# A gated delta-rule layer on one core: the score products take turns with the tile's products and transposes over three PSUM banks

## The chip, the cores and the metric

The kernel runs on one core of one Trainium2 chip. The metric is the device time of one execution in microseconds (us). The kernel before took 4402.71 us, the median of three runs (4402.53 to 4403.26).

## The reference, cut to what matters

The input is `x`, four batches of 1024 tokens with 512 features, in float32. It is normalised, `xn = layernorm(x)`, and two branches work on it:

```
g = silu(ffn(xn))                     # router, two projections, gated MLP
s = attn(xn)                          # below
out = x + s * g

qkvz = xn @ w_qkvz.T                  # 8 key heads, 16 value heads, all of width 128
q, k, v = silu(causal_conv4(q, k, v)) # four taps along the tokens
q, k = q / |q|, k / |k|
S = 0
for each token t:                     # delta rule, one 128x128 state S per value head
    S = S * exp(g_t)
    delta = (v_t - k_t S) * beta_t
    S = S + k_t (outer) delta
    o_t = (q_t * scale) S
s = rmsnorm(o * silu(z)) * norm_weight @ w_out.T
```

## The kernel before, in words

The kernel has two phases. `feed_forward` (the first 1124 us or so) computes the gate `g`, the transposed `xn` (`xt_scratch`) and the decay rates, and leaves them in DRAM. `attention`, the phase that the change touches, computes the rest.

**Tiles, chunks, units.** The heads are worked on in two groups of 4 key heads and 8 value heads. Within a group each batch is cut into tiles of 256 tokens: 32 tiles over all, which this text numbers 0 to 31. A tile has two chunks of 128 tokens, and a chunk has two units of 4 value heads (2 key heads). That is 128 units, four in each tile: units 4q to 4q+3 belong to tile q. The first two units of each batch and group are "fresh": their state is zero, and they skip the steps `recall` and `query`.

**The tile's work on TensorE.** `pe_product` (L1036) multiplies a column block of weights with the tile, in four steps over the contraction: 16 products for the key, query and value heads (L1048) and 4 for `z` (L1052). In float32 each step stands in the trace as two matmuls, so that one product is 8 of them. A product of a key, query or value head lands in a PSUM bank, and the convolution reads it from there: `act_lead` (L1071) writes the first tap, and three times `dve_conv` (L1078) adds a tap. Only then is the bank free. After the convolution and a silu come transposes: `pe_keys` (L1097), `pe_queries` (L1152), `pe_back` (L1138; the keys again, once GpSimd has scaled them at L1132) and `pe_values` (L1181). Each of these is emptied by one step of ScalarE or VectorE.

**Two banks in turn.** The list `fills` has these 30 steps of a tile in their order: 20 products and 10 transposes. Step number i goes to bank i modulo 2, and `bank_for` (L1020) makes it wait until the step two places before it has been emptied. From the first value product on, products and transposes alternate, so that in this stretch each product goes to the same bank as the product before it.

**The scores.** For each unit `pe_scores` (L1234) multiplies keys with keys and keys with queries into a bank of its own, `b_a` (bank 3): 8 matmuls in the trace, at L1244 and L1245. It waits for the keys' second transposes of its tile (`kt_sb`), for the queries' silu, and for the scores of the unit before to be emptied (`kq_sb`). `dve_scores` (L1253) empties the bank into the single buffer `kqm`. It waits for `dve_lower` (L1285) and `dve_attend` (L1292) of the unit before, since they read `kqm`; and `dve_attend` of unit n writes one of three buffers `pt`, so that it waits for `pe_answer` (L1556) of unit n-3. Between scores and lower stand the decays: a scan (L1262) and an exponential on ScalarE (L1270).

**The chains.** From the lower scores of a unit its inverse is built by doubling: GpSimd and ScalarE split the matrix in two fp16 parts (L1297, L1305, L1311), `dve_start` (L1366) starts the chain, and six rounds follow of `pe_level`, `dve_level` (L1378), `pe_merge` and `act_merge` (L1402), then `error`, `first`, `second` and `third`; `dve_third` (L1459) ends it. All their matmuls are short fp16 ones, issued by the helper `each_head` (L1345). Even and odd units have a bank and a chain each (chain 0 and chain 1), and a chain takes its units one after the other. The core of a unit follows: `recall` (L1468), `query` (L1491), `eps` (L1516), `learn` (L1530), `answer` (L1556), and at last `turn` (L1607) and, once in a chunk, `out` (L1622, 8 steps into the bank `b_o`).

**What sets the order.** Each engine's program is written out by `planned` (L813), a list scheduler. It gets lanes (lists whose order is fixed), a duration for each step and, from `after` (L1711), what each step waits for. It runs through a made-up time and lets each engine take, of the steps that are ready, the one with the longest path of steps behind it. On TensorE the lane "pe tile" holds the tiles' products and transposes, and the lane "pe build" the scores; the planner is free in how it puts the two and the chains together. On the chip each engine then runs its list strictly in this order and waits on semaphores.

Some waits tie the tiles to the units: the first tap of the query heads (`act_lead`, query head 0 of tile q) waits until the `query` step of the last unit of tile q-2 is done, since both use `qt[q % 2]`; the silu of `z` waits for the gated output of tile q-2.

Of the kernel before, what the change touches and what calls it, by code (L numbers as in the profile page):

```python
# [29 lines left out]
P = 128  # L30
# [849 lines left out]
def attention(nc, bank, r, x, w_qkvz, w_out, xt_d, g_d, gate_d, row_d, part_d, out):  # L880

    with ExitStack() as ctx:
# [40 lines left out]

        b_o, b_a, b_i0, b_i1, b_s0, b_s1 = bank[2:]
        b_inv = (b_i0, b_i1)
# [52 lines left out]
        def fresh(n):  # L978
# [18 lines left out]
        assert len(fills) % 2 == 0 and Z0 + CPT * NB == NP  # L997
        tile_pe = [(*step, k) for step in fills for k in (range(KT) if step[0] == "product" else (-1,))]
        tile_pe = [step if step[0] == "product" else step[:-1] for step in tile_pe]

        def tile_bank(*step):
            return bank[fills.index(step) % 2]

        def emptied(q, step):

            kind, *i = step
# [12 lines left out]

        def bank_for(pe, q, *step):  # L1020
# [5 lines left out]
            return tile_bank(*step)  # L1026

# [8 lines left out]
        def pe_product(pe, q, i, k):  # L1036
            (kind, h), par = prods[i], q % 2
            if k == 0:
                if i == 0:
                    pe.wait_ge(s[f"x_in{par}"], 16 * (q // 2 + 1))  # L1040
                if q % HALF_TILES == 0 and h == 0:
                    pe.wait_ge(s[f"w{kind}_in"], 16 * (group(q) + 1))
                bank_for(pe, q, "product", i)
            b_p = tile_bank("product", i)
            st = dict(start=(k == 0), stop=(k == KT - 1))
            if kind in "kqv":
                c = W_SPANS[kind][0] + h * P
                j = pe.matmul(b_p[:, 0:WIN], wt[:, k, c:c + P], xtile[:, par, k, :], **st)  # L1048
            else:
                cc, m = divmod(h, NB)  # L1050
                w = wt[:, k, W_SPANS["z"][0] + m * HEADS * P:W_SPANS["z"][0] + (m + 1) * HEADS * P]
                j = pe.matmul(b_p[:], xtile[:, par, k, HALO + cc * P:HALO + (cc + 1) * P], w, **st)  # L1052
            if k == KT - 1:
                j.then_inc(s["pj_ps"], 1)

        def act_lead(act, q, i):
# [5 lines left out]
            if h == 0:  # L1062
# [6 lines left out]
                if kind == "v" and q:  # L1069
                    act.wait_ge(s["vx_ps"], q * UPT)  # L1070
            act.activation(feature(q, i), tile_bank("product", prod_of[i])[:, HALO:HALO + TILE], ACT.Copy, scale=taps[:, group(q), i, HALO:HALO + 1]).then_inc(s["lead"], 1)  # L1071

        def dve_conv(dve, q, i, tap):

            n, done = q * NF + i, ("lead", "cv1", "cv2", "cv")
            acc = feature(q, i)
            dve.wait_ge(s[done[tap]], n + 1)
            dve.scalar_tensor_tensor(out=acc, in0=tile_bank("product", prod_of[i])[:, tap:tap + TILE], scalar=taps[:, group(q), i, tap:tap + 1], in1=acc,  # L1078
                                     op0=ALU.mult, op1=ALU.add).then_inc(s[done[tap + 1]], 1)

        def act_z(act, q, i):
            cc, m = divmod(i, NB)
            act.wait_ge(s["pj_ps"], q * NP + Z0 + i + 1)
            if q >= 2:
                act.wait_ge(s["xf_sb"], (q - 1) * UPT)
            act.activation(zs[:, q % 2, cc, unit_heads(m), :], quad(tile_bank("product", Z0 + i)), ACT.Silu).then_inc(s["zs_sb"], 1)

# [5 lines left out]
        def pe_keys(pe, q, cc):  # L1093
            pe.wait_ge(s["silu"], q * N_SILU + 1)
            b_tr = bank_for(pe, q, "keys", cc)
            for h in range(GK):
# [16 lines left out]
        def dve_keys(dve, q, cc):  # L1113
            n, b_tr = q * CPT + cc, tile_bank("keys", cc)
            dve.wait_ge(s["kx_ps"], n + 1)
# [18 lines left out]
        def pe_back(pe, q, cc):  # L1134
            pe.wait_ge(s["ktok_sb"], q * CPT + cc + 1)
            b_tr = bank_for(pe, q, "back", cc)
            for h in range(GK):
# [3 lines left out]
        def act_back(act, q, cc):  # L1141
            act.wait_ge(s["kb_ps"], q * CPT + cc + 1)
            if q >= 2:
                act.wait_ge(s["kq_ps"], (q - 1) * UPT)
                act.wait_ge(s["ks_ps"], asked((q - 1) * UPT))
            act.activation(kt[:, q % 2, :, cc * P:(cc + 1) * P], quad(tile_bank("back", cc)), ACT.Copy).then_inc(s["kt_sb"], 1)

        def pe_queries(pe, q, cc):
            pe.wait_ge(s["silu"], q * N_SILU + 2)
            b_tr = bank_for(pe, q, "queries", cc)  # L1150
            for h in range(GK):
# [3 lines left out]
        def act_queries(act, q, cc):  # L1155

            n, b_tr = q * CPT + cc, tile_bank("queries", cc)
            act.wait_ge(s["qx_ps"], n + 1)
# [18 lines left out]
        def pe_values(pe, q, m, cc):  # L1177
            pe.wait_ge(s["silu"], q * N_SILU + 3 + m)
            b_tr = bank_for(pe, q, "values", m, cc)
            for h in range(HEADS):  # L1180
# [3 lines left out]
        def act_values(act, q, m, cc):  # L1184
            act.wait_ge(s["vx_ps"], q * UPT + m * CPT + cc + 1)
            if q >= 2:
                act.wait_ge(s["e_ps"], (q - 1) * UPT)
                act.wait_ge(s["r_sb"], asked((q - 1) * UPT))
            act.activation(vtok[:, q % 2, cc, unit_heads(m), :], quad(tile_bank("values", m, cc)), ACT.Copy).then_inc(s["v_sb"], 1)

# [57 lines left out]
        def dve_scores(dve, n):  # L1248
            dve.wait_ge(s["kq_ps"], n + 1)
            if n:  # L1250
                dve.wait_ge(s["lt_sb"], n)
                dve.wait_ge(s["pt_sb"], n)
            dve.tensor_tensor(kqm[:].rearrange("p (t h) c -> p t h c", t=2), b_a[:].rearrange("p (t h c) -> p t h c", t=2, h=KPB),  # L1253
                              mask[:, M_LT:M_LE + 1, :].unsqueeze(2).broadcast_to([P, 2, KPB, P]), ALU.mult).then_inc(s["kq_sb"], 1)
# [417 lines left out]
        for p in range(2):  # L1672
# [21 lines left out]

        def evictions(q, step):

            kind, *i = step
            if kind == "product":
# [3 lines left out]

        lane("pe tile", (("pe", kind, q, *i) for q in tiles for kind, *i in tile_pe))
        lane("act tile", (a for q in tiles for step in fills for a in evictions(q, step) if a[0] == "act"))
        lane("dve tile", (a for q in tiles for step in fills for a in evictions(q, step) if a[0] == "dve"))
        lane("act keys", (("act", "keys", q, cc) for q in tiles for cc in range(CPT)))
# [4 lines left out]
        def after(engine, kind, *i):  # L1711

            at = (engine, kind)
            n = i[0]
            if at in (("pe", "product"), ("pe", "keys"), ("pe", "queries"), ("pe", "back"), ("pe", "values")):
                if kind == "product" and i[2]:
                    return []
                f = fills.index((kind, *i[1:2 if kind == "product" else 3])) - 2
                before = evictions(n - (f < 0), fills[f])
                return before + {"product": [], "keys": [("act", "silu", n, 0)], "queries": [("act", "silu", n, 1)], "back": [("pool", "keys", n, i[1])],  # L1720
                                 "values": [("act", "silu", n, 2 + i[1])]}[kind]
# [30 lines left out]
            if kind == "out":  # L1752
# [4 lines left out]
            return {  # L1757
                ("pe", "scores"): [("dve", "scores", n - 1), ("act", "back", tile, CPT - 1), ("act", "silu", tile, 1)],
                ("dve", "scores"): [("pe", "scores", n)],
# [278 lines left out]
```

## Time and profile before

| | |
|---|---|
| median of three runs | 4402.71 us (4402.53 to 4403.26) |
| the profiled execution | 4402.47 us, span 4400.5 us |
| mean granted TensorE clock | 0.994 |
| TensorE matmul busy | 4294.8 us, 98% of the span |
| VectorE busy | 2838.3 us, 64% |
| ScalarE busy | 2455.4 us, 56% |
| GpSimd busy | 1501.9 us, 34% |
| DMA | mean 35 GB/s |

The span is the time from the first to the last instruction that the profile shows; the execution's own time is 2.0 us more. Matmuls are pipelined: the duration printed for one matmul (say 382 ns) is longer than the distance to the next (some 220 ns), so that a busy share near 100% says that TensorE had no gap, and the distances tell what a matmul costs.

### The profile page before, as it was taken

Reading aid. Unit: us, or ns where it says so; the run is one execution under the profiler, and the core shown is the slowest. Engines: PE = TensorE matmul, PEld = TensorE weight load, DVE = VectorE, ACT = ScalarE, POOL = GpSimd, SP = SyncE. Lnnn points to the kernel's source line nnn. Section 1 sums busy time; section 2 is a strip of 40 time slices with the busy share of each in tenths; the row PEclk is TensorE's granted clock in tenths of the full one; section 3 lists DMA queues with packets and bytes.
Section 4 is the critical chain, followed back from the end, with each engine's and each line's share of the span. In section 5 each row is a group of like instructions: output and inputs, shape, how many; then the busy total and the mean of one; then the engine's idle time right before and its main releaser. Section 6 shows DMA issues by size and latency. Waiting matters only on the chain.

```text
span 4400.5 us, 86630 instructions
## 1 busy us (share of the span) xinstructions
PE 4294.8 (98%) x32312; PEld 3273.7 (74%) x32312; DVE 2838.3 (64%) x6322; ACT 2455.4 (56%) x6251; POOL 1501.9 (34%) x1686
## 2 busy tenths in 40 slices
PE   6999999999899999999999999999999999999998
PEld 5777777777577777777777777777777777777776
DVE  5555555554466666767677766667676776667674
ACT  1222222222466666666667676666666676766675
POOL 2222222222133333333333433334444334433344
PEclk8999999999999999999999999999999999999999
DMA  4000000001200000000000011011111111111111
GB/s 138 31 19 28 30 18 30 21 26 31 96 13 23 23 21 21 21 28 23 21 21 23 23 42 61 21 54 35 42 42 38 36 37 37 35 45 37 35 35 42
DMA packets 114465, 154.71 MB, mean 35 GB/s; under 512 B 32384, under 2 KB 57984, under 8 KB 114048
## 3 DMA queue, kind: packets, MB, share of 16 engines
q1 hardware_dynamic: 77952, 93.94, 6.4%
q10 hardware_dynamic: 36096, 55.24, 4.1%
q8 instruction: 258, 4.23, 0.4%
q14 instruction: 159, 1.30, 0.1%
HBM read 113.73 MB, written 35.42 MB: 34 GB/s over the span
## 4 chain that ended last, share of the span: by engine, by line
PE 69%; DVE 1%; ACT 1%; POOL 1%; issue 1%; POOLq 0%; ACTq 0%; DVEq 0%
PE bank L1048 20%; PE bank L1052 10%; PE bank L1345 10%; PE bank L1622 10%; PE bank L1530 3%; PE bank L1516 2%; PE bank L1556 2%; PE bank L1491 2%; PE bank L1468 2%; PE bank L1244 1%; PE bank L1181 1%; PE bank L1607 1%; PE bank L1245 1%; PE bank L1097 1%; PE bank L1138 1%
## 5 line engine op out<-in xcount | busy, mean ns | idle before, releaser
L1048 PE MATMUL bank<-xtile,wt 128*128 128x259 f32 x4096 | 1092.6, 393 | 21.2 <-DVE vraw L1078 15.8
L1048 PEld LDWEIGHTS bank<-xtile,wt 128*128 128x128 f32 x4096 | 720.5, 191 | 143.1 <-DVE vraw L1078 45.3
L1402 ACT ACTIVATE xyinv<-bank 128x512 f16<-128x512 f32 x768 | 453.2, 593 | 275.5 <-PE bank L1345 272.6
L1622 PE MATMUL bank<-wot,xnt 128*128 128x512 f32 x1024 | 543.5, 621 | 0.8 <-ACT xnt L1615 0.8
L1052 PE MATMUL bank<-wt,xtile 128*128 128x512 f32 x1024 | 524.8, 616 | 0.0
L1378 DVE TENSOR_TENSOR wlev<-bank,mask 128x256 f16<-128x256 f32 x768 | 317.4, 419 | 294.2 <-PE bank L1345 289.3
L439 PE MATMUL bank<-hb,wt 128*128 128x128 f32 x2816 | 376.1, 277 | 42.0 <-DVE part L479 26.8
L1311 POOL TENSOR_TENSOR ltl<-ltm,lth 128x512 f16<-128x512 f32 x128 | 149.2, 1166 | 764.2 <-ACT lth L1305 764.2
L1078 DVE SCALAR_TENSOR_TENSOR vraw<-bank,taps,vraw 128x256 f32<-128x256 f32 x768 | 368.9, 480 | 59.7 <-ACT vraw L1071 41.7
L439 PEld LDWEIGHTS bank<-hb,wt 128*128 128x128 f32 x2816 | 347.0, 192 | 69.7 <-issue 36.9
L1297 POOL TENSOR_TENSOR ltm<-ltm,mask 128x512 f32<-128x512 f32 x128 | 159.1, 1243 | 605.2 <-DVE ltm L1285 605.2
L1345 PEld LDWEIGHTS bank<-xyinv,lth 128*128 128x128 f16 x3584 | 211.7, 97 | 139.9 <-issue 78.3
L516 PE MATMUL bank<-wd_sb,hid 128*128 128x512 f32 x704 | 304.8, 592 | 0.0
L494 ACT ACTIVATE part<-part 128x256 f32<-128x256 f32 x176 | 73.3, 417 | 397.1 <-DVE part L489 396.8
L439 PE MATMUL bank<-hb,comb 128*128 128x128 f32 x2112 | 294.2, 276 | 0.0
L1345 PEld LDWEIGHTS bank<-wlev,xyinv 128*128 128x128 f16 x3072 | 187.2, 97 | 130.8 <-issue 51.1
L502 POOL TENSOR_TENSOR hid<-part 128x256 f32<-128x256 f32 x176 | 128.5, 730 | 414.8 <-ACT part L494 414.8
L1579 POOL TENSOR_TENSOR tq<-tq,zs 128x512 f32<-128x512 f32 x128 | 194.5, 1520 | 213.0 <-DVE tq L1571 195.8
L1345 PE MATMUL bank<-xyinv,lth 128*128 128x64 f16 (+1 forms) x3584 | 258.4, 196 | 8.9 <-ACT xyinv L1402 7.4
L439 PEld LDWEIGHTS bank<-hb,comb 128*128 128x128 f32 x2112 | 265.0, 193 | 0.0
L516 PEld LDWEIGHTS bank<-wd_sb,hid 128*128 128x128 f32 x704 | 132.5, 190 | 160.7 <-issue 153.3
L1587 ACT ACTIVATE osq<-tq 128x128 f16<-128x128 f32 x512 | 151.7, 298 | 129.6 <-POOL tq L1579 129.6
(192 smaller groups left out, 9175.5 us busy)
## 6 DMA issues: line engine op xcount, KB each, us to landing
grows<-row_scratch ACTq DMA_DIRECT2D x126, 256.0 KB, 3.2
xtile<-xt_scratch ACTq DMA_DIRECT2D x30, 518.0 KB, 3.8
xn<-x SPq DMA_DIRECT2D x32, 256.0 KB, 3.9
xt_scratch<-xt SPq DMA_DIRECT2D x16, 512.0 KB, 4.3
g_scratch<-sel SPq DMA_DIRECT2D x32, 256.0 KB, 2.0
part_scratch<-prow SPq DMA_DIRECT2D x32, 256.0 KB, 2.0
prow<-part_scratch SPq DMA_DIRECT2D x32, 256.0 KB, 2.6
sel<-g_scratch SPq DMA_DIRECT2D x32, 256.0 KB, 3.0
```

What stands on the lines that cost most here:

```text
L439: i = pe.matmul(dst, w[:, k, f * P:(f + 1) * P], b[:, k], start=first and k == 0, stop=k == KH - 1, skip_group_check=True)
L516: i = pe.matmul(bank[6 + j % 2][:], hid[:, f, j * P:(j + 1) * P], wd_sb[:, f, :], start=(f == 0), stop=(f == FT - 1))
L1048: j = pe.matmul(b_p[:, 0:WIN], wt[:, k, c:c + P], xtile[:, par, k, :], **st)
L1052: j = pe.matmul(b_p[:], xtile[:, par, k, HALO + cc * P:HALO + (cc + 1) * P], w, **st)
L1078: dve.scalar_tensor_tensor(out=acc, in0=tile_bank("product", prod_of[i])[:, tap:tap + TILE], scalar=taps[:, group(q), i, tap:tap + 1], in1 ...
L1297: pool.tensor_tensor(ltm[:], ltm[:], mask[:, M_NEG, :].unsqueeze(1).broadcast_to([P, HEADS, P]), ALU.subtract).then_inc(s["lti_sb"], 1)
L1345: i = pe.matmul(dst[:, h * cols:(h + 1) * cols], lhsT(h), rhs(h), start=start and h == 0, stop=stop, skip_group_check=True)
L1378: dve.tensor_tensor(wlev[:, lv - 1].rearrange("p h (b t s) -> p h b t s", t=2, s=z)[:, :, :, 0, :], b_inv[p][:, 0:HEADS * P // 2].rearrang ...
L1402: act.activation(dst, b_inv[p][:].rearrange("p (a h b s) -> p a h b s", a=2, h=HEADS, s=z), ACT.Copy).then_inc(s[f"xy_sb{p}"], 1)
L1579: pool.tensor_tensor(tq[:, n % 2], tq[:, n % 2], zs[:, tile % 2, cc, unit_heads(m)], ALU.mult).then_inc(s["xf_sb"], 1)
L1587: i = act.activation(osq[:, h], tq[:, n % 2, h], ACT.Square, accum_out=ssq[:, h:h + 1])
L1622: i = pe.matmul(b_o[:], xnt[:, h], wot[:, h], start=(h == 0), stop=(h == GV - 1))
```

## The change

The bank `b_a` goes, and bank 3 joins banks 0 and 1 in the rotation. The scores become part of `fills`, at four set places, so that a tile has 34 steps: the scores of unit 4(q-1)+1 stand behind the fourth product of tile q, those of unit 4(q-1)+2 behind the first transposes of the queries, those of unit 4(q-1)+3 behind the seventh value product, and those of unit 4q, the first of tile q itself, at the tile's end, behind the last transposes of the values. `turns` is the list of all these steps over all tiles (with one more round at the end for the scores of units 125 to 127); step number i of it goes to bank i modulo 3 of (0, 1, 3), and waits until the step three places before it has been emptied.

For the planner the scores leave their own lane and enter the lane "pe tile", whose order is fixed; `dve_scores` stays in the lane "dve build". No instruction that computes is added or removed.

```diff
-        b_o, b_a, b_i0, b_i1, b_s0, b_s1 = bank[2:]
+        b_o, _, b_i0, b_i1, b_s0, b_s1 = bank[2:]
...
-        fills = [*(("product", i) for i in range(2 * GK)), ("product", V0), ("keys", 0), ("product", V0 + 1), ("keys", 1),
-                 ("product", V0 + 2), ("queries", 0), ("product", V0 + 3), ("queries", 1), ("product", V0 + 4), ("back", 0), ("product", V0 + 5), ("back", 1),
-                 *(("product", V0 + i) for i in range(6, GV)), ("product", Z0), ("product", Z0 + 1), ("values", 0, 0), ("values", 0, 1),
-                 ("product", Z0 + 2), ("product", Z0 + 3), ("values", 1, 0), ("values", 1, 1)]
...
-        def tile_bank(*step):
-            return bank[fills.index(step) % 2]
+        fills = [*(("product", i) for i in range(4)), ("scores", 1), *(("product", i) for i in range(4, 2 * GK)), ("product", V0), ("keys", 0), ("product", V0 + 1), ("keys", 1),
+                 ("product", V0 + 2), ("queries", 0), ("scores", 2), ("product", V0 + 3), ("queries", 1), ("product", V0 + 4), ("back", 0), ("product", V0 + 5), ("back", 1),
+                 ("product", V0 + 6), ("scores", 3), ("product", V0 + 7), ("product", Z0), ("product", Z0 + 1), ("values", 0, 0), ("values", 0, 1),
+                 ("product", Z0 + 2), ("product", Z0 + 3), ("values", 1, 0), ("values", 1, 1), ("scores", 0)]
+        unit_of = lambda q, j: (q - (j > 0)) * UPT + j
+        turns = [(kind, unit_of(q, *i)) if kind == "scores" else (kind, q, *i) for q in range(TILES + 1) for kind, *i in fills
+                 if (0 <= unit_of(q, *i) < UNITS if kind == "scores" else q < TILES)]
+        turn_of = {step: at for at, step in enumerate(turns)}
+        rotated = (bank[0], bank[1], bank[3])
+
+        def tile_bank(kind, *i):
+            return rotated[turn_of[kind, *i] % len(rotated)]
+
+        def emptied(kind, q, *i):
+            if kind == "scores":
+                return [(s["kq_sb"], q + 1)]
...
-            n = q * len(fills) + fills.index(step) - 2
-            if n >= 0:
-                for done in emptied(n // len(fills), fills[n % len(fills)]):
+            at = turn_of[kind, *i] - len(rotated)
+            if at >= 0:
+                for done in emptied(*turns[at]):
                     pe.wait_ge(*done)
...
         def pe_scores(pe, n):
             c, m, tile, cc = where(n)
-            if n:
-                pe.wait_ge(s["kq_sb"], n)
+            b_a = bank_for(pe, "scores", n)
             pe.wait_ge(s["kt_sb"], (tile + 1) * CPT)
             pe.wait_ge(s["silu"], tile * N_SILU + 2)
...
-        lane("pe build", (step for n in units for step in [("pe", "scores", n)]))
...
-        lane("pe tile", (("pe", kind, q, *i) for q in tiles for kind, *i in tile_pe))
+        lane("pe tile", (step for kind, *i in turns for step in ([("pe", kind, *i, k) for k in range(KT)] if kind == "product" else [("pe", kind, *i)])))
```

The other lines of the diff carry the same change into the helpers that read a bank (`tile_bank` gets the tile's number too) and into the planner's table of waits.

## Rows read from the trace of the kernel before

**Rows 1.** The page: busy time of each engine, share of the span, instructions.
```profile
PE 4294.8 (98%) x32312; PEld 3273.7 (74%) x32312; DVE 2838.3 (64%) x6322; ACT 2455.4 (56%) x6251; POOL 1501.9 (34%) x1686
```
**Rows 2.** Busy time by stretch: length, then busy us of PE, PEld, DVE, ACT, POOL, and clock.
```profile
1126.80:1201.40 74.60, 60.90 (x275) 43.33 (x276) 40.38 (x79) 39.56 (x91) 14.01 (x13) 0.93 0.16 53
...
2684.00:2785.50 101.50, 101.50 (x813) 77.62 (x812) 70.56 (x154) 69.09 (x178) 36.30 (x39) 1.00 0.08 29
4202.00:4317.00 115.00, 113.90 (x1076) 91.27 (x1076) 93.45 (x203) 86.77 (x227) 54.08 (x57) 1.00 0.12 40
4317.00:4401.00 84.00, 73.09 (x503) 47.65 (x501) 35.11 (x82) 36.26 (x102) 35.99 (x39) 0.94 0.12 42
```
**Rows 3.** TensorE's waits from 1126 to 1300 us: total, times, longest.
```profile
PE bank L1048 <- DVE vraw L1078: 9.8, 6, 2.2
...
PE bank L1048 <- DVE qt L1078: 2.1, 3, 1.0
PE bank L1181 <- ACT zs L1086: 1.9, 1, 1.9
...
PE bank L1048 <- DVE kraw L1078: 0.6, 2, 0.3
```
**Rows 4.** TensorE's waits from 1300 to 4200 us, the three longest.
```profile
PE bank L1345 <- ACT xyinv L1402: 7.0, 15, 0.7
PE bank L1048 <- DVE vraw L1078: 6.0, 9, 1.3
PE bank L1097 <- DVE qt L1078: 0.8, 1, 0.8
```
**Rows 5.** TensorE in tile 0, in order of time: start, length, and idle time before.
```profile
1150.42 3.21 PE L1048 MATMUL bank<-xtile,wt 128*128 128x259 f32 x8 [2.24 <-DVE vraw L1078]
...
1159.90 2.02 PE L1048 MATMUL bank<-xtile,wt 128*128 128x259 f32 x8 [1.69 <-DVE vraw L1078]
...
1171.33 0.49 PE L1244 MATMUL bank<-kt 128*128 128x128 f32 x2 [0.69 <-ACT kt L1146]
...
1176.82 7.03 PE L1052 MATMUL bank<-wt,xtile 128*128 128x512 f32 x16
...
1189.18 8.46 PE L1052 MATMUL bank<-wt,xtile 128*128 128x512 f32 x16
```
**Rows 6.** VectorE around the scores of unit 60, in order of time.
```profile
2670.31 0.68 DVE L1292 TENSOR_TENSOR pt<-gam,kqm 128x512 f32<-128x512 f32 x1
...
2674.94 0.65 DVE L1253 TENSOR_TENSOR kqm<-bank,mask 128x512 f32<-128x512 f32 x1
...
2690.43 0.42 DVE L1366 TENSOR_TENSOR xyinv<-lth,mask 128x512 f16<-128x512 f16 x1
```
**Rows 7.** The chain that ended last, within tile 16: start, length, what.
```profile
2684.99 0.88 PE bank L1048 x4
2685.87 0.22 PE bank L1345 x4
...
2693.54 0.52 PE bank L1048 x2
...
2783.50 0.45 PE bank L1345 x8
```
**Rows 8.** VectorE: start and end of chain 0's unit 0, and of its unit 124.
```profile
1180.12 0.42 DVE L1366 TENSOR_TENSOR xyinv<-lth,mask 128x512 f16<-128x512 f16 x1
...
1231.30 0.68 DVE L1459 SCALAR_TENSOR_TENSOR yfin<-bank,xyinv 128x512 f32<-128x512 f32 x1
...
4282.68 0.43 DVE L1366 TENSOR_TENSOR xyinv<-lth,mask 128x512 f16<-128x512 f16 x1
...
4317.56 0.69 DVE L1459 SCALAR_TENSOR_TENSOR yfin<-bank,xyinv 128x512 f32<-128x512 f32 x1 [0.94 <-PE bank L1345]
```
**Rows 9.** TensorE: the query of unit 3, and the scores of unit 60.
```profile
1286.45 1.02 PE L1491 MATMUL bank<-state,qt 128*128 128x256 f32 x4
...
2642.61 0.39 PE L1244 MATMUL bank<-kt 128*128 128x128 f32 x2
```

More of the change, by code:

```diff
@@ L1042, in pe_product @@
                     pe.wait_ge(s[f"w{kind}_in"], 16 * (group(q) + 1))
-                bank_for(pe, q, "product", i)
-            b_p = tile_bank("product", i)
+                bank_for(pe, "product", q, i)
+            b_p = tile_bank("product", q, i)
             st = dict(start=(k == 0), stop=(k == KT - 1))
@@ L1070, in act_lead @@
                     act.wait_ge(s["vx_ps"], q * UPT)
-            act.activation(feature(q, i), tile_bank("product", prod_of[i])[:, HALO:HALO + TILE], ACT.Copy, scale=taps[:, group(q), i, HALO:HALO + 1]).then_inc(s["lead"], 1)
+            act.activation(feature(q, i), tile_bank("product", q, prod_of[i])[:, HALO:HALO + TILE], ACT.Copy, scale=taps[:, group(q), i, HALO:HALO + 1]).then_inc(s["lead"], 1)
         def dve_conv(dve, q, i, tap):
@@ L1077, in dve_conv @@
             dve.wait_ge(s[done[tap]], n + 1)
-            dve.scalar_tensor_tensor(out=acc, in0=tile_bank("product", prod_of[i])[:, tap:tap + TILE], scalar=taps[:, group(q), i, tap:tap + 1], in1=acc,
+            dve.scalar_tensor_tensor(out=acc, in0=tile_bank("product", q, prod_of[i])[:, tap:tap + TILE], scalar=taps[:, group(q), i, tap:tap + 1], in1=acc,
                                      op0=ALU.mult, op1=ALU.add).then_inc(s[done[tap + 1]], 1)
@@ L1085, in act_z @@
                 act.wait_ge(s["xf_sb"], (q - 1) * UPT)
-            act.activation(zs[:, q % 2, cc, unit_heads(m), :], quad(tile_bank("product", Z0 + i)), ACT.Silu).then_inc(s["zs_sb"], 1)
+            act.activation(zs[:, q % 2, cc, unit_heads(m), :], quad(tile_bank("product", q, Z0 + i)), ACT.Silu).then_inc(s["zs_sb"], 1)
         def act_silu(act, q, j):
@@ L1094, in pe_keys @@
             pe.wait_ge(s["silu"], q * N_SILU + 1)
-            b_tr = bank_for(pe, q, "keys", cc)
+            b_tr = bank_for(pe, "keys", q, cc)
             for h in range(GK):
@@ L1113, in dve_keys @@
         def dve_keys(dve, q, cc):
-            n, b_tr = q * CPT + cc, tile_bank("keys", cc)
+            n, b_tr = q * CPT + cc, tile_bank("keys", q, cc)
             dve.wait_ge(s["kx_ps"], n + 1)
@@ L1135, in pe_back @@
             pe.wait_ge(s["ktok_sb"], q * CPT + cc + 1)
-            b_tr = bank_for(pe, q, "back", cc)
+            b_tr = bank_for(pe, "back", q, cc)
             for h in range(GK):
@@ L1145, in act_back @@
                 act.wait_ge(s["ks_ps"], asked((q - 1) * UPT))
-            act.activation(kt[:, q % 2, :, cc * P:(cc + 1) * P], quad(tile_bank("back", cc)), ACT.Copy).then_inc(s["kt_sb"], 1)
+            act.activation(kt[:, q % 2, :, cc * P:(cc + 1) * P], quad(tile_bank("back", q, cc)), ACT.Copy).then_inc(s["kt_sb"], 1)
         def pe_queries(pe, q, cc):
             pe.wait_ge(s["silu"], q * N_SILU + 2)
-            b_tr = bank_for(pe, q, "queries", cc)
+            b_tr = bank_for(pe, "queries", q, cc)
             for h in range(GK):
@@ L1155, in act_queries @@
         def act_queries(act, q, cc):
-            n, b_tr = q * CPT + cc, tile_bank("queries", cc)
+            n, b_tr = q * CPT + cc, tile_bank("queries", q, cc)
             act.wait_ge(s["qx_ps"], n + 1)
@@ L1178, in pe_values @@
             pe.wait_ge(s["silu"], q * N_SILU + 3 + m)
-            b_tr = bank_for(pe, q, "values", m, cc)
+            b_tr = bank_for(pe, "values", q, m, cc)
             for h in range(HEADS):
@@ L1188, in act_values @@
                 act.wait_ge(s["r_sb"], asked((q - 1) * UPT))
-            act.activation(vtok[:, q % 2, cc, unit_heads(m), :], quad(tile_bank("values", m, cc)), ACT.Copy).then_inc(s["v_sb"], 1)
+            act.activation(vtok[:, q % 2, cc, unit_heads(m), :], quad(tile_bank("values", q, m, cc)), ACT.Copy).then_inc(s["v_sb"], 1)
         def load_tile(dma, q):
@@ L1693, in attention, with evictions @@
         lane("pool out", (("pool", "out", c) for c in chunks[HALF_CHUNKS:]))
-        def evictions(q, step):
-            kind, *i = step
+        def evictions(kind, q, *i):
+            if kind == "scores":
+                return [("dve", "scores", q)]
             if kind == "product":
@@ L1701, in evictions @@
             return [("dve" if kind == "keys" else "act", kind, q, *i)]
-        lane("pe tile", (("pe", kind, q, *i) for q in tiles for kind, *i in tile_pe))
-        lane("act tile", (a for q in tiles for step in fills for a in evictions(q, step) if a[0] == "act"))
-        lane("dve tile", (a for q in tiles for step in fills for a in evictions(q, step) if a[0] == "dve"))
+        lane("pe tile", (step for kind, *i in turns for step in ([("pe", kind, *i, k) for k in range(KT)] if kind == "product" else [("pe", kind, *i)])))
+        lane("act tile", (a for step in turns for a in evictions(*step) if a[0] == "act"))
+        lane("dve tile", (a for step in turns if step[0] != "scores" for a in evictions(*step) if a[0] == "dve"))
         lane("act keys", (("act", "keys", q, cc) for q in tiles for cc in range(CPT)))
@@ L1714, in after @@
             n = i[0]
-            if at in (("pe", "product"), ("pe", "keys"), ("pe", "queries"), ("pe", "back"), ("pe", "values")):
+            if at in (("pe", "product"), ("pe", "keys"), ("pe", "queries"), ("pe", "back"), ("pe", "values"), ("pe", "scores")):
                 if kind == "product" and i[2]:
                     return []
-                f = fills.index((kind, *i[1:2 if kind == "product" else 3])) - 2
-                before = evictions(n - (f < 0), fills[f])
+                f = turn_of[kind, *(i[:2] if kind == "product" else i)] - len(rotated)
+                before = evictions(*turns[f]) if f >= 0 else []
+                if kind == "scores":
+                    tile = where(n)[2]
+                    return before + [("act", "back", tile, CPT - 1), ("act", "silu", tile, 1)]
                 return before + {"product": [], "keys": [("act", "silu", n, 0)], "queries": [("act", "silu", n, 1)], "back": [("pool", "keys", n, i[1])],
@@ L1757, in after @@
             return {
-                ("pe", "scores"): [("dve", "scores", n - 1), ("act", "back", tile, CPT - 1), ("act", "silu", tile, 1)],
                 ("dve", "scores"): [("pe", "scores", n)],
```

12 lines of the change are left out of this document (4 added, 8 removed).

## The prediction

> **What bounds the kernel now.** I read the page's busy times first, then the busy times by stretch, then TensorE's waits, and at last single stretches in order of time. The page says TensorE: 4294.8 us busy of 4400.5, with VectorE at 64% and the others below [rows 1]. An average of 98% can hide a stage with another limit, so the stretches come next. In tile 16 TensorE is busy 101.50 us of 101.50 at the full clock [rows 2]. The waits say the same of the whole middle: from 1300 to 4200 us they name 7.0 us on the chains' evictions, 6.0 us on convolutions and 0.8 us more, in 2900 us [rows 4]. In steady state the order of TensorE's work doesn't matter, since it works without a gap, and only its amount does.
>
> That leaves two places. Tile 0 (1126.8 to 1201.4 us) has 60.90 us busy in 74.60, at a clock of 0.93 [rows 2]: nothing but the tile's own work exists yet, and with two banks it waits for evictions. The end, from 4317 us, has 73.09 us busy in 84.00 [rows 2].
>
> Time of the profiled execution: span 4400.5 plus 2.0 around it, 4402.5 us; the median of the runs is 4402.7, so the two can be used as one.
>
> **The change part by part.**
>
> *Bank waits in tile 0 and the start of tile 1.* With two banks a product waits for the one two steps back; where products and transposes alternate, that is the product just before it, so that product and convolution follow each other: 1.69 us of idle time after each pair of a product and its transposes [rows 5]. With three banks the product waits for a transpose instead. TensorE needs 1.8 us for a product and 0.4 for the transposes between, VectorE three additions of 0.5, so TensorE sets the pace. What goes: 9.8 (values) + 2.1 (queries) + 0.6 (keys) + 1.9 (the values' transposes behind the silu of z) = 14.4 us [rows 3]. Nothing hides this today, since no other work exists there. What is late next is the keys' way back through GpSimd. I estimate 0.7 us of wait for it, about as much as the wait of the first scores that goes, so the two cancel.
>
> *The clock.* Eight matmuls of a product took 3.21 us instead of 2.02 behind the 2.24 us of idle time, and sixteen of z took 8.46 instead of 7.03 [rows 5]: behind two of those gaps TensorE ran at its lower level, 1.2 GHz in place of 2.4, for a while. Both gaps go, and with them 1.2 + 1.4 = 2.6 us.
>
> The Trainium skill bears on that: "TensorE: Matmul & The Clock Gate", section "A second HAM failure mode: psum-queue depth-cycling", says that cycling through PSUM banks can leave TensorE idle so often that its clock swings. The trace agrees for tile 0 (0.93) and not for tile 16 (1.00) [rows 2]. By that rule the gain would be the same 2.6 us, not a share of the whole kernel.
>
> *Bank waits in the middle.* 6.0 + 0.8 us [rows 4]. A wait for a convolution is shorter with a third bank only where VectorE was late by less than one more step of TensorE; where VectorE took other work first, it stays. I take half, 3.4 us; the bounds are 0 and 6.8.
>
> *The scores in their turn.* The same 8 matmuls for each unit, so no work is added. Two waits are new. First, the scores' bank must now be emptied within three steps. Behind the waiting step stands all of TensorE's list, chains too. In the middle the scores of unit 60 were issued at 2642.61 [rows 9] and emptied only at 2674.94, right behind `attend` of unit 59 at 2670.31 [rows 6], which waited for the answer of unit 56. In the new order these scores come at the end of the tile, at about 2681 on the old scale (tile 16's products run at 2684.99 [rows 7]), and the third step behind them some 3.5 us later. `attend` is by then 14 us back: that slack covers the wait, which costs 0. Second, the chain: unit 60 started at 2690.43 [rows 6]. From scores (1171.33 [rows 5]) to start (1180.12 [rows 8]) unit 0 needed 9 us, so that 2681 just does. The other three scores of a tile come 7 to 20 us ahead of their need. Cost in the middle: 0, bounds 0 and 1 us in each of 29 tiles.
>
> *The start of the pipeline.* The scores of unit 0 now stand behind all of tile 0. From the terms above tile 0 shrinks to about 50 us and they are issued near 1176 us, against 1171.33 before [rows 5]: 5 us later. The tiles, however, run some 17 us earlier, and the first tap of tile 2's query heads waits for the query of unit 3, which ended near 1287 [rows 9]. Between lie chain 0's units 0 and 2. Unit 0 took 1180.12 to 1231.30, 51 us; unit 124, late in the kernel, took 4282.68 to 4317.56, 35 us [rows 8]. So there are 16 us to be had in unit 0 alone if TensorE serves the chain sooner. If it does, the 17 us are kept; if not, tile 2 waits for about 5 + 17 = 22 us, less the two products that the banks can take in advance, 18 us. I take 3 us lost, since the planner serves the longest path first and this one has become it; the bounds are 0 and 18.
>
> *The end.* The scores of units 124 to 127 now come behind all of tile 31; before, those of 126 and 127 already stood among its last products. Tile 31's products lose their freedom to lie beside the last chains. Against that, its products must come first and leave the `out` steps for later, so there is still work to fill the chains with. From the start of unit 124 (4282.68) the end was 118 us away, of which the two chains take two units each, 35 us and up. At best these begin at the same distance and meet less traffic (6 us gained); at worst they begin 12 us later. I take 3 us lost.
>
> *Short stretches.* TensorE's list is written anew. A pair of matmuls costs 0.44 us behind its like (0.88 for four) and 0.52 right behind the chains' fp16 ones, and tile 16 has 51 such stretches (the first and the last are in [rows 7]). A tile has 64 chain steps (4 units of 6 levels, 6 merges and 4 more), so the number could rise to 64 or fall by a few. 0.08 us each in 30 tiles: 13 more cost 31 us, 4 fewer give 10. I take 0, since the chains keep their length, their number and their gaps.
>
> Sum: -14.4 - 2.6 - 3.4 + 3 + 3 = -14.4 us, 4402.5 - 14.4 = 4388 us.
>
> **The rivals.**
>
> *A: the head start is given back.* All the gain is made before 1240 us. If the middle is set by the units and not by TensorE's work, tile 2 waits and the kernel is where it was: 4402.5 - 2.6 - 3.4 + 3 = 4399.5 to 4403. For it: the wait of the first tap on the query of two tiles before is real, and the scores of unit 0 do come later. Against it: TensorE has no gap from tile 2 on [rows 2, 4], so what is saved in front of a full engine should stay saved. The Trainium skill has a sentence on this side: the same page, in "HAM oscillation — how this bites in real kernels", reports a matmul kernel to which PSUM double-buffering "gave no further gain". By it the time would be 4402.
>
> *B: slower, by more and shorter fp16 stretches.* The tiles' path of steps gets shorter with three banks, and it now carries the scores. The planner then puts the chains' steps ahead more often, each as soon as it is ready, in place of two at a time between products. The place is every tile of the middle, the price 0.08 us for each stretch. With all 64 apart it is 31 us, and the time is 4388 + 31 = 4419; it decides against the change from about 6 more in each tile (14.4 / (0.08 x 30)). For it: of the 51 stretches 18 hold a single step of four matmuls, 33 hold more, so there is something to break up. Against it: the chains' steps are ready at moments that ScalarE and VectorE set, and these engines' work is the same.
>
> *C: the new wait at the scores holds TensorE.* If the answers come some 14 us later against the tile than today, each unit's scores block the list. At 1 us for a tile this is +29, 4417 us; 0.5 us gives 4402. Against it stands the slack of rows 6.
>
> *D: a long tail.* Only the last item at its worst and more: the four last units, 25 us without work beside them, 4388 + 22 = 4410 us.
>
> **How the numbers follow.** What a measurement of this kernel can tell from no change is 0.2%, 9 us. I give the forecast 0.55, A 0.19, B 0.10, C 0.06, D 0.04, and 0.06 that fewer stretches and a shorter end bring more than I took (4375). Forecast and the last make faster 0.61. Same: A and the milder part of C, 0.21. Slower: the rest, 0.18. For the range: the largest gain of all bounds is 14.4 + 2.6 + 6.8 + 6 + 10, 40 us, but these don't come together; 4374 leaves little out. Upward it takes in A whole and the smaller half of B and C: 4412.
>
> **What would show it.** Right: tile 0 without the waits at L1048, and the first product of tile 1 near 1177 us in place of 1200; tiles of 101 us in the middle; VectorE's `attend` some 10 us ahead of the scores of each tile's end. Wrong: waits of TensorE on L1253 at a product (C); a gap near the fifth product of tile 2 (A); four-matmul stretches of L1345 in larger number and tiles of 102 us (B); over 20 us of gaps behind the last product (D). A wrong sign in the length of the middle tiles would turn the forecast over, since one of 0.5 us in each of 30 tiles equals the whole gain.

## The result, and the profile after

The changed kernel takes 4365.43 us (median of 4 runs, 4364.83 to 4366.52), the kernel before 4402.68 us beside it. The ratio is 0.9915, with a 95% interval of 0.9898 to 0.9933: faster by 37 us. The forecast was 4388, with 4374 to 4412 as its range. The direction was right and the size was not: the time lies below the range.

The page after, next to [rows 1]:

```profile
span 4363.3 us, 86631 instructions
PE 4284.3 (98%) x32312; PEld 3255.0 (75%) x32312; DVE 2813.6 (64%) x6322; ACT 2467.2 (57%) x6252; POOL 1561.1 (36%) x1686
```

The span fell by 37.2 us, TensorE's busy time by 10.5. The rest is idle time that is gone. To see where, I cut both traces at the same points of the work: where tile 0's products begin, where those of tile 2 begin, where those of tile 30 begin, and the end. Below stand the busy times of the kernel before in these three stretches (columns as in [rows 2]; the last stretch stands first):

```profile
4095.30:4400.50 305.20, 293.69 (x2457) 220.45 (x2455) 201.22 (x444) 195.07 (x513) 134.06 (x141) 0.98 0.12 39
1126.80:1269.00 142.20, 124.32 (x769) 92.25 (x770) 81.92 (x165) 79.16 (x192) 30.64 (x30) 0.96 0.10 32
1269.00:4095.30 2826.30, 2811.89 (x22507) 2143.77 (x22506) 1964.57 (x4214) 1912.62 (x4921) 1054.14 (x1111) 1.00 0.10 32
```

and of the changed one:

```profile
4055.70:4363.30 307.60, 295.13 (x2467) 220.98 (x2465) 200.13 (x446) 190.96 (x511) 139.32 (x142) 0.98 0.12 38
1126.60:1251.40 124.80, 119.74 (x757) 89.11 (x758) 79.93 (x162) 73.78 (x184) 25.73 (x25) 0.97 0.11 37
1251.40:4055.70 2804.30, 2804.30 (x22508) 2127.41 (x22507) 1943.61 (x4216) 1933.78 (x4931) 1112.36 (x1113) 1.00 0.10 32
```

| | before | after | difference | forecast |
|---|---|---|---|---|
| tiles 0 and 1 | 142.2 | 124.8 | -17.4 | -17.0 |
| tiles 2 to 29 | 2826.3 | 2804.3 | -22.0 | -3.4, and +3 for the filling |
| tiles 30 and 31, to the end | 305.2 | 307.6 | +2.4 | +3 |

The work before tile 0 gives the last 0.2 us. So the start and the end came as forecast, and the middle, which I had nearly written off, brought more than the start. TensorE is busy there for 2804.30 us of 2804.30. The list of its waits in the changed kernel from 1300 to 4160 us is empty, where the kernel before had [rows 4] and a fourth row of 0.6 us:

```profile
core 0 of [0], span 4363.3 us
engine line waited for: us in total, times, longest us
```

In tile 0 of the changed kernel the pairs of a product and its transposes now follow each other without the 1.69 us of [rows 5]. In order of time:

```profile
1144.71 2.02 PE L1052 MATMUL bank<-xtile,wt 128*128 128x259 f32 x8
1146.57 0.61 PE L1101 MATMUL bank<-con,kraw 128*128 128x128 f32 x4
1147.06 2.02 PE L1052 MATMUL bank<-xtile,wt 128*128 128x259 f32 x8
1148.94 0.63 PE L1156 MATMUL bank<-con,qt 128*128 128x128 f32 x4
...
1157.07 0.63 PE L1142 MATMUL bank<-con,ktok 128*128 128x128 f32 x4 [0.57 <-DVE vraw L1082]
```

The last row's 0.57 us is the one wait of note left in tile 0. Tile 1's products begin at 1177.6 us.

### The profile page after: what moved, and what is told of

Same layout as the page of the kernel before. It is cut to its first block, busy times and chain, and to the rows that moved or that the text cites. A ratio compares the mean times of both kernels' runs of the same rounds, so it can differ in the third digit from the quotient of the medians.

```text
span 4363.3 us, 86631 instructions
## 1 busy us (share of the span) xinstructions
PE 4284.3 (98%) x32312; PEld 3255.0 (75%) x32312; DVE 2813.6 (64%) x6322; ACT 2467.2 (57%) x6252; POOL 1561.1 (36%) x1686
## 4 chain that ended last, share of the span: by engine, by line
PE 71%; POOL 1%; issue 0%; ACT 0%; DVE 0%; POOLq 0%; DVEq 0%
PE bank L1052 20%; PE bank L1348 11%; PE bank L1625 10%; PE bank L1056 10%; PE bank L1559 3%; PE bank L1533 3%; PE bank L1519 3%; PE bank L1471 2%; PE bank L1494 2%; PE bank L1247 1%; PE bank L1610 1%; PE bank L1248 1%; PE bank L1185 1%; PE bank L1142 1%; PE bank L1101 1%; PE bank L1156 1%
## 5 line engine op out<-in xcount | busy, mean ns | idle before, releaser
L1052 PE MATMUL bank<-xtile,wt 128*128 128x259 f32 x4096 | 1103.8, 392 | 4.3 <-PEq L643 2.5
L1056 PE MATMUL bank<-wt,xtile 128*128 128x512 f32 x1024 | 534.9, 615 | 0.0
L1381 DVE TENSOR_TENSOR wlev<-bank,mask 128x256 f16<-128x256 f32 x768 | 315.1, 416 | 269.6 <-PE bank L1348 268.3
L1325 POOL TENSOR_TENSOR kend<-ktok,gts 128x256 f32<-128x256 f32 x256 | 157.1, 635 | 625.4 <-issue 625.4
L1582 POOL TENSOR_TENSOR tq<-tq,zs 128x512 f32<-128x512 f32 x128 | 221.6, 1731 | 191.1 <-DVE tq L1574 160.4
L1300 POOL TENSOR_TENSOR ltm<-ltm,mask 128x512 f32<-128x512 f32 x128 | 171.2, 1338 | 312.0 <-DVE ltm L1288 312.0
```

Source lines behind the costliest of these rows:

```text
L1300: pool.tensor_tensor(ltm[:], ltm[:], mask[:, M_NEG, :].unsqueeze(1).broadcast_to([P, HEADS, P]), ALU.subtract).then_inc(s["lti_sb"], 1)
L1325: i = pool.tensor_tensor(kend[:, r * REP:(r + 1) * REP], ktok[:, tile % 2, cc, m * KPB + r].unsqueeze(1).broadcast_to([P, REP, P]), rate(t ...
L1381: dve.tensor_tensor(wlev[:, lv - 1].rearrange("p h (b t s) -> p h b t s", t=2, s=z)[:, :, :, 0, :], b_inv[p][:, 0:HEADS * P // 2].rearrang ...
L1582: pool.tensor_tensor(tq[:, n % 2], tq[:, n % 2], zs[:, tile % 2, cc, unit_heads(m)], ALU.mult).then_inc(s["xf_sb"], 1)
```

## The experiments

Each ran beside the kernel before, on one chip; the median of the kernel before in the three groups was 4402.46, 4404.41 and 4404.88 us.

### The set places without the third bank

```diff
 def tile_bank(kind, *i):
-    return rotated[turn_of[kind, *i] % len(rotated)]
+    return bank[3] if kind == "scores" else bank[row_of[kind, *i] % 2]
```

`row_of` counts products and transposes alone; the waits follow suit, on the chip and in the planner.

> The scores stand at the four set places in the tile's lane, but keep a bank of their own; products and transposes rotate over two banks as before. Theory (the third bank is the gain: TensorE needs a product that is ready whenever the chains have nothing for it): no gain, 4400 us or more, tile 0 with the same 1.7 us gaps behind each product and transpose, gaps in the tiles with fresh units as before or larger. Rival (the set places are the gain, since late scores leave VectorE and TensorE free for the chains): 4370 to 4385 us, gaps only in tile 0.

Measured: 4527.14 us, ratio 1.0283 (1.0268 to 1.0299). The rival is out: the set places alone are no gain but a loss of 125 us. That it would be so large neither theory had said. TensorE's waits from 1300 to 4300 us, the three longest:

```profile
PE bank L1354 <- ACT xyinv L1411: 39.9, 37, 2.8
PE bank L1058 <- DVE vraw L1088: 28.4, 53, 1.1
PE bank L1058 <- DVE qt L1088: 16.0, 28, 0.6
```

The last two are waits for a bank. The first is one of the chains, and the next experiment but one says what it means. A plain tile (one without fresh units) takes 104.3 to 108.1 us in place of 101.2. Why set places cost so much with two banks wasn't tested by itself. It may be that a chain now starts only when the tile's list, with its bank waits, has come to the scores.

### Scores in turn over two banks

```diff
-rotated = (bank[0], bank[1], bank[3])
+rotated = (bank[0], bank[1])
```

> The change with two banks in rotation in place of three: scores, products and transposes take turns over banks 0 and 1, and bank 3 is unused. Theory: slower than the kernel before, 4415 us or more, since every wait for an eviction of before stays and the scores now hold one of the two banks. Rival (sharing in turn is the gain, not the number of banks): 4365 to 4395 us.

Measured: 4546.96 us, ratio 1.0328 (1.0311 to 1.0345). To share costs 20 us more than an own bank at the same places. At the same places and the same sharing, the third bank is worth 4547 - 4365 = 182 us. That doesn't make the whole gain its own: with three banks and the scores at their old places the kernel is slower than before as well (below), so that neither half of the change is a gain without the other.

### A list planned for two banks, run over three

```diff
 f = turn_of[kind, ...] - len(rotated)
 before = evictions(*turns[f]) if f >= 0 else []
+before += [a for step in last_in_bank(kind, ...) for a in evictions(*step)]
```

The planner gets the two-bank waits on top; on the chip the banks and the waits are those of the change.

> TensorE's and the other engines' lists are planned as if products and transposes had two banks (and the scores their turn among three), but the chip runs them over three banks, as in the change. If the third bank works through the order that it allows (my theory): the time stays near that of the kernel with set places and an own bank, at most the 14 us of waits in tile 0 and 1 better. Rival (it works at run time, by waits that are no longer met, whatever the order): 4365 to 4375 us, like the change.

Measured: 4513.95 us, ratio 1.0251 (1.0236 to 1.0267), 13 us better than with two banks on the chip as well. The rival had 4365 to 4375. TensorE's waits from 1300 to 4300 us, the three longest:

```profile
PE bank L1355 <- ACT xyinv L1412: 66.6, 35, 3.3
PE bank L1355 <- DVE wlev L1388: 16.8, 35, 1.8
PE bank L1632 <- ACT xnt L1625: 7.3, 28, 0.3
```

This is the run that taught me most. The waits for convolutions at the products, 44 us in the run with the set places alone, are gone, and nothing is won in the middle: the same idle time now stands under the chains' evictions, 66.6 + 16.8 us in place of 39.9 + 4.1. The two traces can be compared step by step, since TensorE has its 32312 matmuls in exactly the same order in both; from tile 2 to tile 29 they take 2930.1 us here and 2931.0 there, and 2804.3 in the change. TensorE runs its list in order. Where the list has a chain step next, as I read it since the planner found no product whose bank was free, TensorE waits for the chain, and the profile names the chain. So the third bank works mostly through the list that it allows (4514 - 4365 = 149 us), and by the waits met on the chip nearly in tile 0 alone (57.0 us in place of 67.0).

The counterpart, the change's own list with two banks on the chip, wasn't tried. I would expect it to stand still, since a convolution in VectorE's list can come behind a step that waits for the product after it.

### Two runs without fresh units

If the waits for chains in [rows 4] were such gaps, they should vanish when TensorE has more to do. They stood in the tiles with fresh units, where it has 3.5 us less. (The stretch of time in which tile q's products run holds the units of tile q-1, so that in the middle these are tiles 5, 9 and so on to 29.)

```diff
 def asked(n):
-    return n - NB * (n // UPB) - min(n % UPB, NB)
+    return n - min(n, NB)
 def fresh(n):
-    return n % UPB < NB
+    return n < NB
```

> The kernel before, but only the first two units of all are fresh: the first units of the seven later batches run recall and query too, on the state of the batch before (the state is not reset, so this part of the computation differs). That is 1.74 us of TensorE work for each of 14 units, 24.4 us. Theory (the gaps of the tiles with fresh units, shown as waits for the chains, were TensorE without ready work, since both banks were held): the added work fills them, each of the seven tiles comes to the 101.2 us of its neighbours, 708.4 us in place of 699.1: 4412 us. Rival (the gaps belong to the chains, whatever else there is to do): all of 24.4 us is added, 4427 us.

> The changed kernel with the same edit: the same 14 units run recall and query on the state of the batch before. Both theories: its seven tiles with fresh units had no gaps (97.7 us each) and come to the 101.0 us of the others, +23 us: 4388 us. The distance to the kernel before with the same edit is then 24 us by the theory (in place of 37), 38 by the rival.

Measured: 4413.82 us (1.0020, 1.0010 to 1.0029) and 4388.85 us (0.9964, 0.9951 to 0.9978); 4412 and 4388 were expected by the theory, 4427 for the first by the rival. Beside each other the two kernels with the edit are 25.0 us apart, where the theory had 24 and the rival 38. Of 24.4 us of added work the kernel before pays 9.4, the changed one 22 to 23 (its medians come from two groups, 23.4 apart; its spans are 22.4 apart). Tile 5 of the kernel before, without and with the edit:

```profile
1574.20:1673.40 99.20, 98.02 (x794) 74.42 (x793) 67.84 (x142) 66.05 (x169) 35.91 (x40) 1.00 0.06 20
```

```profile
1576.00:1677.20 101.20, 101.20 (x810) 77.39 (x809) 70.22 (x155) 69.12 (x178) 35.59 (x39) 1.00 0.08 22
```

The gap is gone with the added work, in all seven such tiles, and what is left of the waits from 1300 to 4200 us in the edited kernel stands in tiles 3 and 4:

```profile
PE bank L1048 <- DVE vraw L1078: 1.3, 2, 1.0
PE bank L1097 <- DVE qt L1078: 0.8, 1, 0.8
PE bank L1345 <- DVE xyinv L1372: 0.6, 1, 0.6
PE bank L1345 <- ACT xyinv L1402: 0.2, 1, 0.2
```

Of the 7.0 us under L1402, 6.8 went, though no chain was touched. So the gaps were TensorE out of ready work.

### The scores at their old places

> The change with the scores at the places which they had in the kernel before (behind product 6, behind the first value product, behind the keys' first way back, and the first unit of the tile behind the keys' second way back). Theory A (the third bank is all, places matter little): 4365 to 4380 us. Theory B (a place is good only if VectorE is about to need the scores; in the kernel before those of a tile's first unit lay 32 us in their own bank, which in a rotation blocks the third product behind them): 4400 us or more, with waits of TensorE on dve_scores or a delayed product behind the scores of the tile's first unit.

```diff
-fills = [... product 3, scores 1, product 4 ... queries 0, scores 2, ... product V6, scores 3, ... values 1 1, scores 0]
+fills = [... product 5, scores 1, product 6 ... product V0, scores 2, keys 0, ... back 0, scores 3, product V5, back 1, scores 0, ...]
```

Measured: 4440.42 us, ratio 1.0084 (1.0069 to 1.0099). Theory A is out. With three banks the old places lose 75 us to the new ones, and the kernel is 38 us slower than before. Theory B had the time, but not the wait that it named: TensorE waits on `dve_scores` once in the whole run, for 1.4 us. The waits from 1300 to 4200 us are mostly under the chains once more:

```profile
PE bank L1348 <- DVE wlev L1381: 25.8, 24, 1.3
PE bank L1348 <- DVE errl L1449: 13.9, 28, 0.6
PE bank L1101 <- DVE qt L1082: 7.5, 24, 0.3
```

In order of time, around unit 56 in this run: TensorE's scores and the answer of unit 52, then VectorE's `attend` of unit 55 and the scores of unit 56.

```profile
2547.76 0.46 PE L1247 MATMUL bank<-kt 128*128 128x128 f32 x2
...
2550.95 1.05 PE L1559 MATMUL bank<-reps,pt 128*128 128x128 f32 x8
...
2552.14 0.69 DVE L1295 TENSOR_TENSOR pt<-gam,kqm 128x512 f32<-128x512 f32 x1 [1.18 <-PE bank L1559]
...
2553.08 0.68 DVE L1256 TENSOR_TENSOR kqm<-bank,mask 128x512 f32<-128x512 f32 x1
```

Three of these four steps in the changed kernel, where `attend` of unit 55 is 10.8 us ahead of VectorE's scores:

```profile
2541.31 0.68 DVE L1295 TENSOR_TENSOR pt<-gam,kqm 128x512 f32<-128x512 f32 x1
...
2550.70 0.44 PE L1247 MATMUL bank<-kt 128*128 128x128 f32 x2
...
2552.14 0.68 DVE L1256 TENSOR_TENSOR kqm<-bank,mask 128x512 f32<-128x512 f32 x1
```

At the old place the scores' bank, written at 2547.76, comes free only behind the answer of the unit four before, 5.3 us later; in the change it is held for 1.4 us. My reading is that this ties the tile's list to the units', so that it can't run ahead of them. No run tested that by itself; the next one tests how much of the loss the place of these scores carries.

### Only the first unit's scores at the new place

```diff
-..., ("back", 1), ("scores", 0), ...]
+..., ("back", 1), ..., ("values", 1, 1), ("scores", 0)]
```

(against the run before; the other three stay at the old places)

> Three banks, the scores of a tile's second, third and fourth unit at the places of the kernel before, those of its first unit at the tile's end as in the change. Theory (what hurt with the old places was the first unit's scores, 32 us ahead of their use, holding one bank of three and with it VectorE's list): most of the 75 us between the old places and the change comes back, 4365 to 4385 us. Rival (all four places matter alike): near the middle, 4390 to 4420 us.

Measured: 4392.73 us, ratio 0.9975 (0.9965 to 0.9985). The time misses the theory's range and lies at the lower edge of the rival's. Neither has it whole: 48 of the 75 us come back with the one place, and the other three hold 27 together, which is not alike. In the middle this run has 6.9 us of waits at L1381 and 56 short stretches in a plain tile (102.2 us) where the change has 51 (101.1). A matmul of a product right behind such a stretch costs some 0.075 us more (0.295 against 0.220 us from one to the next). Five more are 0.4 of the 1.1 us.

### Earlier scores in the first tile, and in the last

```diff
-..., product Z1, values 0 0, ..., values 1 1, scores 0]
+..., product Z1, scores 0, values 0 0, ..., values 1 1]
...
+for n, behind in ((0, ("product", 0, V0 + 7)), (1, ("product", 0, Z0 + 1)), (2, ("values", 0, 1, 1)), (3, ("product", 1, 3))):
+    turns.remove(("scores", n))
+    turns.insert(turns.index(behind) + 1, ("scores", n))
```

> The change with the scores of a tile's first unit four transposes and two products of z earlier (behind the second product of z), and with the first four units' scores sooner: unit 0 behind the last value product of tile 0, unit 1 behind the second product of z, unit 2 at the end of tile 0, unit 3 behind the fourth product of tile 1. Theory: the middle has no gap left to win, so that only the start (4.3 us of gaps in tile 1) and the end (6.7 us) can give something: 4356 to 4365 us. Rival (an earlier place blocks a bank again, as the old places do): above 4370 us.

Measured: 4357.04 us, ratio 0.9893 (0.9878 to 0.9908), at the good end of the theory. The gaps of tile 1 are gone, and 0.8 us is left at the start. Tiles 0 and 1, the middle and the end of this run:

```profile
1127.30:1242.40 115.10, 114.30 (x729) 86.61 (x729) 79.83 (x161) 75.71 (x188) 28.35 (x28) 0.99 0.12 37
1242.40:4047.90 2805.50, 2805.35 (x22537) 2135.83 (x22535) 1951.59 (x4217) 1922.84 (x4934) 1104.46 (x1113) 1.00 0.11 33
4047.90:4354.00 306.10, 294.27 (x2467) 220.59 (x2465) 202.73 (x444) 189.86 (x507) 136.78 (x141) 0.99 0.12 38
```

The first half of the edit alone (the scores of each tile's first unit behind the second product of z):

> The change with one step moved: the scores of a tile's first unit stand behind the second product of z in place of the tile's end, in every tile; the first tile is as in the change otherwise. If the 8 us that the version with an early first tile gained came from the start alone, this one gains only what unit 0's earlier scores give there, 1 to 4 us on the change: 4361 to 4365 us, with middle tiles of 101.0 to 101.2 us. Rival (the place in each tile counts too): 4357 us, like the version with both edits.

Measured: 4360.03 us, ratio 0.9900 (0.9885 to 0.9915). Between the two expectations, 1 us below the first. The intervals are too wide to part the two versions by their times; their traces show tile 1 at 69.1 us here, 62.1 with both halves and 73.8 in the change, and the same 101.1 us for a plain tile. So the gain was made at the start.

At last the last four units' scores were put among the last tile's products as well:

```diff
+(124, ("product", 31, V0 + 7)), (125, ("product", 31, Z0 + 1)), (126, ("product", 31, Z0 + 3)), (127, ("values", 31, 1, 1))
```

> The version with an early first tile, and the scores of the last four units among the last tile's products (unit 124 behind its last value product, 125 behind the second product of z, 126 behind the fourth, 127 at the end). If the end loses because the last scores come behind all products (my term of 3 us): 3 us better than that version, 4354 us. Rival (the end is set by the two chains' length and by the last output): no difference, 4356 to 4358 us.

Measured: 4353.85 us, ratio 0.9887 (0.9871 to 0.9904). The span of the profiled execution is 3.5 us shorter than with the first tile alone: tile 31 to the end is 2.8 us shorter (202.4 in place of 205.2), near the 3 us of my term, and the rest lies ahead of tile 0. The clock has a part in it: the version with the first tile alone has a stretch at 1.2 GHz near 4340 us that this one has not. The two medians, 3.2 us apart in different groups, are no proof by themselves. This is the fastest version, 1.1% below the kernel before.

## Why the forecast was wrong

**Tiles 0 and 1: right.** -14.4 for bank waits and -2.6 for the clock were forecast, -17.4 measured. The split is less clean, so that the close match of the sum is partly luck: the gaps of both tiles gave 12.9 us (from 17.9 to 5.0, with 4.3 us of new ones in tile 1 that I had not named), and busy time gave the rest. The two stretches at 1.2 GHz behind the gaps of tile 0 went; one new one stands at 1216 us, behind two gaps of 0.96 and 0.57 us.

**The filling of the pipeline (+3): too dear.** Tile 2 takes 98.7 us after and 98.2 before, without a gap, so that the wait which I had priced didn't come. Rival A is out with it.

**Bank waits in the middle (-3.4): this step failed.** The measured term is -22.0. I took from [rows 4] only the rows that named a convolution, 6.8 us, and halved them; a fourth row of 0.6 us I had left out. The 7.0 us under "ACT xyinv" I took for the chains' own latency, out of the change's reach. The run planned for two banks shows that such a wait is what a lack of banks looks like in an engine that runs a fixed list, and the runs without fresh units show that these very 7 us were of this kind. All 14.4 us of gaps in tiles 2 to 29 went. So did 7.6 us of busy time (2811.9 to 2804.3): 1.7 us of them a stretch at the lower clock behind one of those gaps, at 3650 us (last section). What the other 5.9 us are isn't shown; they come as up to 0.15 us in most plain tiles, 0.3 in one with fresh units, and more in tiles 3 and 4.

The Trainium skill has a rule that would have pointed there: "Perfetto Trace Analysis", section "Optimization Strategy", says that the same gap coming back again and again on the engine that should be full can mean too little SBUF or PSUM for the next tile. The trace agrees: the gap came back in each of the seven tiles with fresh units and went with the third bank. The Trainium skill's sentence on "no further gain" from PSUM double-buffering ("TensorE: Matmul & The Clock Gate", section "HAM oscillation — how this bites in real kernels"), which I had cited for rival A, tells of another kernel; in this one the third bank, with the scores moved, gave 37 us.

Behind the failed step stood the sentence that in steady state only the amount of work matters. It holds for the plain tiles (101.2 us before, 101.1 after) and not for the seven tiles with fresh units, which took 99.2 to 101.9 us before and take 97.7 now: 15.1 us of the 22. I had read one plain tile of [rows 2] and no other. The bounds of this term, 0 to 6.8, were drawn from the rows that carried its name, and this made the whole range too narrow. That the direction was right is no luck: the start alone brought 17.4 us, against 0.5 lost in tile 2 and 2.4 at the end.

**The new wait at the scores (0): right.** No wait of the changed kernel names L1256. `attend` stands 10.8 us ahead of the scores at a tile's end, 14 and "some 10" were said. Rival C did not happen here. Its wait at the scores didn't show with the old places either (once, 1.4 us), though a bank that the scores hold for longer went with a loss of 75 us there.

**The end (+3): right,** +2.4, and the last version takes it back. Rival D is out.

**Short stretches (0): nearly right.** A plain tile has 51 before and after (52 in some early ones). But each of the seven tiles with fresh units went from 49 to 53, and tiles 2 to 29 have 34 more in all; at 0.075 us each that would be some 2.6 us, well hidden in the gain. Rival B, with 31 us, is out.

## What to carry to other kernels

Where an engine runs a planned list in order, the profile names what the next step in the list waited for, and that is often not what was scarce: ask of every gap why nothing else stood there, and count it as removable if a buffer would have let something stand there. Read one tile of each kind before a steady state is called full; the rare kind held two thirds of the middle's gain here. And in a shared rotation the places count as much as the banks: the same three banks went with -37 us where each scores product is emptied some 2 us after it is issued, and with +38 us where the list has the scores of a tile's first unit a third of a tile earlier, among others.

## What the hardware showed that I had not expected

The same three gaps (0.3, 0.7 and 1.3 us, with chain steps between) came three times in the kernel before, at 3242, 3646 and 4052 us. Behind the second TensorE ran at 1.2 GHz for 3.4 us, behind the others it did not. The first product behind the gaps at 3242 and at 3646 us:

```profile
3244.90 1.58 PE L1048 MATMUL bank<-xtile,wt 128*128 128x259 f32 x6 [1.27 <-DVE vraw L1078]
3648.74 2.12 PE L1048 MATMUL bank<-xtile,wt 128*128 128x259 f32 x6 [1.27 <-DVE vraw L1078]
```

A stretch behind each, the later one first, with the granted clock behind POOL's figures:

```profile
3649.60:3653.00 3.40, 3.40 (x19) 2.57 (x18) 1.62 (x4) 1.07 (x2) 0.00 (x0) 0.51 0.53 181
3245.60:3249.00 3.40, 3.40 (x45) 3.07 (x44) 2.79 (x6) 2.24 (x5) 0.00 (x0) 1.00 0.46 161
```

The stretch at the lower level made its tile 1.7 us longer than the other two (101.9 in place of 100.2). In tile 1 of the changed kernel such a stretch stands behind gaps of 0.96 and 0.57 us, at 1213 and 1214 us; the changed kernel without fresh units has the same two gaps and keeps its full clock there (tile 1 takes 72.1 us in place of 73.8). So gaps of 1.5 us together can cost twice their length, but need not.
